# Attention scores from two 64-row halves of the TensorE array instead of 128-row products with q high and low stacked

## The reference, cut to what matters

```python
q, k, v = jnp.split(h @ wqkv, 3, axis=-1)          # 8 heads of 64
q = l2norm(q) * qs; k = l2norm(k) * ksc
q, k = rotary_xpos(q, k)
# local attention: a window of 128 queries sees its own 128 keys and the 128 before
sim = jnp.einsum('bhwid,bhwjd->bhwij', bq, bk)     # 64 products per score
attn = jax.nn.softmax(jnp.where(mask, -max, sim), axis=-1)
out = jnp.einsum('bhwij,bhwjd->bhwid', attn, bv)
```

## Time and profile before

| | |
|---|---|
| median of 3 runs | 3440.58 us (3440.16 to 3442.09) |
| span of the profiled execution | 3440.9 us (0.3 us above the median) |
| mean granted clock of PE | 0.976 of full |
| busy share PE / DVE / ACT / POOL | 93% / 86% / 67% / 55% |
| stretch of the loop over slots | about 860 to 3400 us |

### The profile page before, as it was taken

One profiled execution on the slowest core, in us unless ns is written; L12 is line 12 of the kernel. 1 busy time (PEld: TensorE's weight loads), 2 busy tenths in 40 slices (PEclk: granted clock), 3 DMA queues, 4 the chain that ended last, 5 costly groups with the idle time before them and its releaser, 6 DMA issues.

```text
span 3440.9 us, 85961 instructions
## 1 busy us (share of the span) xinstructions
PE 3200.0 (93%) x24600; PEld 2670.4 (78%) x24600; DVE 2975.0 (86%) x8121; ACT 2315.4 (67%) x5021; POOL 1876.9 (55%) x2307
## 2 busy tenths in 40 slices
PE   6999999973999999999999999999999999999997
PEld 3666667672888888888888888888888888888886
DVE  6888787857899989988989989998998999899995
ACT  5435353503787777777777777877777777777774
POOL 2433333335665655655655656666665566666662
PEclk9999999985999999999999999999999999999999
DMA  1111111134111111111111111111111111111111
GB/s 35 46 52 41 56 37 55 40 119 140 35 43 40 37 40 41 41 41 41 37 40 45 37 45 38 41 55 43 43 45 46 46 43 43 44 45 51 46 45 36
DMA packets 205536, 163.08 MB, mean 47 GB/s; under 512 B 25646, under 2 KB 203282, under 8 KB 204946
## 3 DMA queue, kind: packets, MB, share of 16 engines
q1 hardware_dynamic: 205330, 161.06, 15.3%
HBM read 106.44 MB, written 54.54 MB: 47 GB/s over the span
## 4 chain that ended last, share of the span: by engine, by line
DVE 24%; issue 18%; PE 18%; ACT 12%; POOL 1%; DVEq 1%; ACTq 1%; DMA 0%; SPq 0%; POOLq 0%
PE b_ps L898 4%; DVE b_probs L1173 4%; PE b_ps L948 3%; ACT b_probs L1021 3%; PE b_ps L870 2%; DVE b_kT_low L1123 2%; DVE b_probs L1160 2%; ACT b_gl L1036 2%; ACT L1021 2%; PE b_ps L886 2%; DVE b_qT L1120 2%; PE b_ps L913 2%; PE b_ps L914 2%; DVE b_t L1062 2%; ACT b_qT L987 2%
## 5 line engine op out<-in xcount | busy, mean ns | idle before, releaser
L870 PE MATMUL b_ps<-b_wqkv,b_hT_hi 128*128 128x512 f32 x1536 | 503.4, 409 | 43.2 <-DVE b_qT L1120 42.2
L1222 POOL TENSOR_TENSOR b_rstd<-b_var,b_mhalf 128x1 f32<-128x1 f32 x128 | 72.2, 564 | 821.1 <-DVE b_var L1134 821.1
L1021 ACT ACTIVATE b_probs<-b_probs,b_negmax 128x256 f32<-128x256 f32 x1024 | 505.6, 495 | 5.7 <-DVE b_negmax L1160 3.3
L948 PE MATMUL b_ps<-b_h2T,b_w 128*128 128x256 f16 x4224 | 474.2, 273 | 0.7 <-ACT b_h2T L979 0.7
L948 PEld LDWEIGHTS b_ps<-b_h2T,b_w 128*128 128x128 f16 x4224 | 414.5, 98 | 49.3 <-ACT b_h2T L979 0.9
L1212 POOL TENSOR_TENSOR b_sq<-b_sq 128x512 f32<-128x512 f32 (+5 forms) x768 | 418.1, 544 | 58.2 <-ACT b_sq L1000 17.9
L1173 DVE TENSOR_SCALAR b_probs<-b_probs,b_rinv 128x256 f32<-128x256 f32 x1024 | 424.8, 456 | 18.1
L1244 POOL TENSOR_TENSOR b_rn<-b_ss_min,b_mhalf 128x16 f32<-128x16 f32 x128 | 379.2, 2963 | 34.9 <-DVE b_ss_min L1071 33.3
L870 PEld LDWEIGHTS b_ps<-b_wqkv,b_hT_hi 128*128 128x128 f32 x1536 | 281.0, 193 | 114.8 <-DVE b_qT L1120 57.8
L442 PE MATMUL a_ps<-a_xs,a_E 128*128 128x256 f16 x3072 | 345.2, 273 | 4.1 <-POOL a_xs L233 4.0
L959 PE MATMUL b_ps<-b_w,b_hid 128*128 128x256 f32 x1536 | 342.2, 379 | 1.2 <-DVE b_hid L1196 1.2
(11 more groups left out here) (136 smaller groups left out, 7305.4 us busy)
## 6 DMA issues: line engine op xcount, KB each, us to landing
b_hx<-xs_dram SPq DMA_DIRECT2D x256, 64.0 KB, 1.9
b_rot<-rot_dram SPq DMA_DIRECT2D x128, 128.0 KB, 2.1
b_xr<-xs_dram SPq DMA_DIRECT2D x128, 128.0 KB, 2.1
xp_dram<-b_xp SPq DMA_DIRECT2D x128, 128.0 KB, 1.7
b_h<-xp_dram SPq DMA_DIRECT2D x256, 64.0 KB, 1.8
a_xn<-in_L_attn_x_dram SPq DMA_DIRECT2D x20, 512.0 KB, 3.8
a_x_res<-in_L_attn_x_dram SPq DMA_DIRECT2D x66, 128.0 KB, 2.1
x_dram<-a_x SPq DMA_DIRECT2D x64, 128.0 KB, 1.7
```

The source lines that it names most:

```text
L870: last = nc.tensor.matmul(ps[:, bank, :], hT[:, k, :], wqkv[:, ds(layer(s), 1), part, k, bank * INNER:(bank + 1) * INNER], start=(k == 0 a ...
L948: last = nc.tensor.matmul(ps[:, bank, half * 2 * P:(half + 1) * 2 * P], w1[:, ds(layer(2 * j), 1), wp, k, first:first + P], h2T[:, hp, k, ...
L1021: nc.scalar.activation(probs[:, h, :], probs[:, h, :], ACT.Exp, bias=negmax[:, h:h + 1], scale=-1.0, accum_out=rowsum[:, h:h + 1]).then_in ...
```

## The change

The high and low parts of q and k are kept in four full-width tiles, one entry for each pair of heads, with one head in the upper 64 partitions and the other in the lower. There is no stacking, no copy across halves, and no zeros. Each head's scores come from three products of 64 rows. The two heads of a pair are issued one after the other, one in the upper and one in the lower half of the array's rows, and they write to different PSUM banks. So the heads are placed anew: bank 3 holds heads 0 and 2, bank 4 heads 1 and 3, bank 5 heads 4 and 6, bank 6 heads 5 and 7, and PE reports scores after every second pair instead of every pair. Waits for the banks follow (`BANK_READ`).

```diff
+BANK_READ = {3: 3, 4: 4, 5: 7, 6: 8}
...
-            kT = sb("kT", [P, HEADS, 2 * P], F32R)
-            kT_low = sb("kT_low", [P, HEADS, 2 * P], F32R)
+            kT, kT_low = sb("kT", [P, HP, 2 * P], F32R), sb("kT_low", [P, HP, 2 * P], F32R)
...
-            qT = sb("qT", [P, HEADS, P], F32R)
+            qT, qT_low = sb("qT", [P, HP, P], F32R), sb("qT_low", [P, HP, P], F32R)
...
+            def head_scores(h):
+
+                bank, column = 3 + 2 * (h // 4) + h % 2, (h // 2) % 2
+                return ps[:, bank, column * 2 * P:(column + 1) * 2 * P]
...
-                        pe.wait_ge(kT_lo, 2 * (t + 1))
-                        pe.wait_ge(kT_both, 2 * (t + 1))
-                        pe.wait_ge(qT_lo, 2 * (t + 1))
+                        pe.wait_ge(kT_lo, t + 1)
+                        pe.wait_ge(qT_lo, t + 1)
                         for p in range(HP):
-                            for h in range(2):
-
-                                scores = ps[:, 3 + p, h * 2 * P:(h + 1) * 2 * P]
-                                nc.tensor.matmul(scores, qT[:, 2 * p + h, :], kT[:, 2 * p + h, :], start=True, stop=False)
-                                last = nc.tensor.matmul(scores, qT[:, 2 * p + h, :], kT_low[:, 2 * p + h, :], start=False, stop=True)
-                            last.then_inc(scores_done, 1)
+                            for a, (q_part, k_part) in enumerate(((qT, kT), (qT, kT_low), (qT_low, kT))):
+                                for h, rows in enumerate(half_rows):
+                                    last = nc.tensor.matmul(head_scores(2 * p + h), q_part[rows, p, :], k_part[rows, p, :], start=(a == 0), stop=(a == 2))
+                            if p % 2 == 1:
+                                last.then_inc(scores_done, 1)
...
-                        for h, rows in enumerate(half_rows):
-                            nc.scalar.copy(qT[rows, h::2, :], by_pair(ps[rows, 2, :])).then_inc(qT_hi, 1)
+                        nc.scalar.copy(qT[:], by_pair(ps[:, 2, :])).then_inc(qT_hi, 1)
                         act.wait_ge(kT_done, t + 1)
                         par = (r - 1) % 2
-                        for h, rows in enumerate(half_rows):
-                            nc.scalar.copy(kT[rows, h::2, par * P:(par + 1) * P], by_pair(ps[rows, 6, :])).then_inc(kT_hi, 1)
-                        for h, rows in enumerate(half_rows):
-                            act.wait_ge(kT_hi, 2 * t + h + 1)
-                            nc.scalar.copy(kT[half_rows[1 - h], h::2, par * P:(par + 1) * P], kT[rows, h::2, par * P:(par + 1) * P]).then_inc(kT_both, 1)
+                        nc.scalar.copy(kT[:, :, par * P:(par + 1) * P], by_pair(ps[:, 6, :])).then_inc(kT_hi, 1)
...
-                        for h, rows in enumerate(half_rows):
-                            dve.wait_ge(qT_hi, 2 * t + h + 1)
-                            nc.vector.tensor_tensor(qT[half_rows[1 - h], h::2, :], by_pair(ps[rows, 2, :]), qT[rows, h::2, :], ALU.subtract).then_inc(qT_lo, 1)
-                        for h, rows in enumerate(half_rows):
-                            dve.wait_ge(kT_hi, 2 * t + h + 1)
-                            nc.vector.tensor_tensor(kT_low[rows, h::2, par * P:(par + 1) * P], by_pair(ps[rows, 6, :]), kT[rows, h::2, par * P:(par + 1) * P],
-                                                    ALU.subtract).then_inc(kT_lo, 1)
+                        dve.wait_ge(qT_hi, t + 1)
+                        nc.vector.tensor_tensor(qT_low[:], by_pair(ps[:, 2, :]), qT[:], ALU.subtract).then_inc(qT_lo, 1)
+                        dve.wait_ge(kT_hi, t + 1)
+                        nc.vector.tensor_tensor(kT_low[:, :, par * P:(par + 1) * P], by_pair(ps[:, 6, :]), kT[:, :, par * P:(par + 1) * P],
+                                                ALU.subtract).then_inc(kT_lo, 1)
...
-                            wait_apart(dve, scores_done, HP * t + p + 1, passed_dve)
+                            if p % 2 == 0:
+                                wait_apart(dve, scores_done, 2 * t + p // 2 + 1, passed_dve)
```

More of the change, by code:

```diff
@@ L735, in phase_b @@
                 "kT_done", "qT_done", "kT_hi", "kT_lo", "qT_hi", "qT_lo"))
-            kT_both = sem("kT_both")
             scores_done, mask_ready = sem("scores_done"), sem("mask_ready")
@@ L862, in run @@
                             if bank == 2:
-                                wait(pe, qT_lo, 2 * s)
+                                wait(pe, qT_lo, s)
                             else:
@@ L882, in run @@
                             if p == HP - 1 and in_range(s - 1):
-                                pe.wait_ge(kT_lo, 2 * s)
+                                pe.wait_ge(kT_lo, s)
                             pe.wait_ge(probs_ready, HEADS * t + 2 * p + 2)
@@ L942, in run @@
                             if bank > 2 and in_range(s - 1):
-                                pe.wait_ge(scores_kept, HEADS * (s - 1) + 2 * (bank - 3) + 2)
+                                pe.wait_ge(scores_kept, HEADS * (s - 1) + BANK_READ[bank])
                             for half in range(1 if c == FULL else 2):
@@ L955, in run @@
                         if in_range(s - 1):
-                            pe.wait_ge(scores_kept, HEADS * (s - 1) + 2)
+                            pe.wait_ge(scores_kept, HEADS * (s - 1) + BANK_READ[3])
                         for n in range(2):
@@ L984, in run @@
                         act.wait_ge(qT_done, t + 1)
-                        wait(act, scores_done, HP * t)
-                        for h, rows in enumerate(half_rows):
-                            nc.scalar.copy(qT[rows, h::2, :], by_pair(ps[rows, 2, :])).then_inc(qT_hi, 1)
+                        wait(act, scores_done, 2 * t)
+                        nc.scalar.copy(qT[:], by_pair(ps[:, 2, :])).then_inc(qT_hi, 1)
                         act.wait_ge(kT_done, t + 1)
                         par = (r - 1) % 2
-                        for h, rows in enumerate(half_rows):
-                            nc.scalar.copy(kT[rows, h::2, par * P:(par + 1) * P], by_pair(ps[rows, 6, :])).then_inc(kT_hi, 1)
-                        for h, rows in enumerate(half_rows):
-                            act.wait_ge(kT_hi, 2 * t + h + 1)
-                            nc.scalar.copy(kT[half_rows[1 - h], h::2, par * P:(par + 1) * P], kT[rows, h::2, par * P:(par + 1) * P]).then_inc(kT_both, 1)
+                        nc.scalar.copy(kT[:, :, par * P:(par + 1) * P], by_pair(ps[:, 6, :])).then_inc(kT_hi, 1)
                     if in_range(s):
@@ L1157, in run @@
                                 floor_norms(s)
-                            wait_apart(dve, scores_done, HP * t + p + 1, passed_dve)
+                            if p % 2 == 0:
+                                wait_apart(dve, scores_done, 2 * t + p // 2 + 1, passed_dve)
                             for h in range(2 * p, 2 * p + 2):
-                                nc.vector.tensor_tensor_reduce(probs[:, h, :], ps[:, 3 + p, (h % 2) * 2 * P:(h % 2 + 1) * 2 * P], which,
+                                nc.vector.tensor_tensor_reduce(probs[:, h, :], head_scores(h), which,
                                                                rn[:, (r - 1) % 2, h:h + 1], ABOVE_ALL, ALU.add, ALU.min,
```

## The result

The changed kernel takes 3271.52 us (median of 4 runs, 3270.43 to 3272.43) against 3441.04 us, a ratio of 0.9507 with a 95% interval from 0.9494 to 0.9521. The forecast was 3302 us, and the range 3272 to 3392. The direction was right.

What follows compares the result with a forecast made beforehand. PE was taken as the bound, idle 105 us of its loop in short stalls that begin on DVE and ACT. Stalls of 102 us plus 36 us of score work made 138 us off 3440.9: 3302 us, range 3272 to 3392.

Steps and rivals of the forecast that it cites:

- The bound, and what each instruction costs: Loop: PE bounds with short stalls begun by DVE and ACT; a half-width cast or subtraction costs as much as full width.
- Halves at once: Score products: the two 64-row products of a pair run at once, 0.118 us a pair, with 0.235 as the other bound.
- the likeness to L898: Product with v, split by columns: two products run at once and loads run in pairs; taken as model for 0.118 us.
- rivals 1 and 2: Score pairs: halves take turns, 0.235 us a pair, 3484 us, chance 0.15; or overlap in part, 0.16, 3367 us, chance 0.10.
- The score block: Score products on PE: 1.72 us instead of 2.00, 0.28 less over 128 slots, 36 us gained.
- the second change of the array's division: From halves to the full array ahead of L837: new cost of 0.1 to 0.2 us, taken as 0.2.
- The jump: Loop jump: qkv product at L886 starts 1.47 us earlier after each of 31 jumps, 46 us gained.
- D: Time DVE begins L1120 after the loop's jump, 2004.51 in the trace; claimed to move along with PE.
- the even slots of the second layer: L886 in even slots not following a jump: 0.64 us of idle time and lost overlap, 14 times, 9 us gained.
- Odd slots: L886 to L898 and L898 itself: ACT's copies keep pace, 0.48 us in some 60 slots, 29 us gained.
- L837 in the second layer: Wait of L837 in odd slots: 0.6 us of idle time and lost overlap in 29 slots, 18 us gained.
- Rival 3: Whole loop: other waits replace those removed; with only half of the 102 us back, 3353 us; chance 0.13.

Runs made afterwards that it cites:

- e1: The changed kernel with all 12 score products of the upper rows issued first, then all 12 of the lower; 3401.12 us.
- g1: The changed kernel with 14 DVE semaphore increments ahead of the first loop and 24 between the loops, so only the first loop has the stop; 3267.76 us.
- f2: The changed kernel with 38 DVE semaphore increments between the two loops, none in a loop; no stop in either loop; 3254.65 us.
- e4: The changed kernel with 4 more DVE semaphore increments in every slot, 16 in each loop body and 32 ahead of the first; 3291.27 us.
- e2: The changed kernel with each DVE subtraction done for the two halves again; 3386.89 us.
- f1: The new score products alone: the changed kernel with DVE's subtractions and ACT's casts in halves again and two more ACT copies; 3398.23 us.
- f4: The kernel before with 100 DVE semaphore increments ahead of the first loop and 119 between the loops; only the second loop lost its stop; 3411.16 us.
- f3: The changed kernel with 14 DVE semaphore increments ahead of the first loop; stop in the first loop, two stops in the second; 3305.20 us.

## Why the prediction was wrong, by its steps

**The bound, and what each instruction costs: right.** PE is the bound, and it was found idle for 25 us, forecast near 30. A cast takes 587 ns in full width and took 582 in half width, a subtraction 690 and 689. No L994 is left, and L841 and L890 hardly wait for DVE.

**Halves at once: right**, and the likeness to L898 carried it. Pairs come every 0.113 or 0.118 us, e1 shows what turns would have cost, and rivals 1 and 2 are out. TensorEngine Tiling (Array Packing) of the Trainium skill says under Key Properties that tiles load and multiply in parallel. The trace agrees: the two loads of a pair begin 3 ns apart, and so do its two products. The 24 loads don't queue up. (The prediction calls 24 loads a third more than 16. They are half more; its sum doesn't use it.)

**The score block: right in kind, too small in size.** It is 1.61 us (median) and not 1.72. The mis-sized term is the second change of the array's division: from the last pair to the first product of L841 it takes 0.22 us, so about 0.1 beyond a pair's distance and not the 0.2 I put in. A pair was sized rightly. The block gives 47 us instead of 36.

**The jump: this is the step that failed.** The prediction said that DVE begins at D, 2.86 us late, and that D moves along with PE, and so it took the stop as fixed. In the first loop it went altogether. It depends on where the loop's body lies in DVE's program, and the change, with fewer DVE instructions ahead of that body and in it, left it without the stop. That is worth 13 us (g1 against f2). With the stop the change would have taken about 3285 us, inside the range. e4, which has both stops, takes 3291. Nothing of the rows before told of this, except that the 2.86 us had "issue" as their reason.

The sum of this step had a second error, which hid the first in part. I multiplied by 31 jumps, and there are 25; 25 x 1.47 is 37 us and not 46. Each jump gave more than 1.47, though. With both stops in place (e4), the qkv block behind a jump lost 1.63 us in the first loop and 1.75 in the second, 42 us in all. Without the first loop's stop it is 54. That 42 is near 46 is luck.

The stop alone is not the whole surplus of 32 us: the jumps give 8 more than forecast, odd and even slots 11 more, the score block 11 more, other blocks 2. Each term but those of L837 and of the even slots of the second layer (9 us, as forecast) was too small, and together they passed the lower end of the range.

**Odd slots: right in kind, too small.** Transposes and the product with v lost 0.40 + 0.16 us in odd slots, not 0.48, and 0.05 in even ones: 40 us in all against 29. Why the even ones got shorter isn't shown.

**L837 in the second layer: right.** Before, the score blocks of the second half took 145 us against 127 in the first; now they take 104 against 103. The 18 us of difference were forecast and are gone.

**Rival 3, stalls handed on: no.** But e2 shows that it was near. With the old work on DVE, 59 us of waits for the attention output came in place of the shorter score block. The prediction counted savings of DVE and ACT only against waits that stood in the profile before, and left out those that the faster PE would have made. The change brings the faster PE and the savings at once, so these waits never appear and the sum came near, though its account of what each part is worth was wrong: it gave the products 36 us by themselves, and alone they give 13 (f1 against f4).

## What to carry to other kernels

When one engine is dense and two others are close behind, sum up waits for the change as a whole; don't price its parts one by one, since each part's worth depends on the others (11 or 59 us for the same work on ACT). If a head's 64 channels leave half the array's rows empty, put the two heads of a pair into the row halves, with neighbouring instructions in different halves: grouped by half, the same products took 2.65 us instead of 1.61. (Here neighbours also write to different banks; no run varied that.) And where an engine stops behind a loop's jump with "issue" as the reason, try to move the body by some instructions before believing a comparison of one per cent: f2 and f3, the same loops moved by 38 and 14 instructions, lie 51 us or 1.5% apart.

## What the runs showed of the hardware that I had not expected

- DVE's stop behind a jump (2.5 us) depends on where the body lies in its program. The same body, 38 instructions on, had none; 14 instructions on it stopped twice, for 2.2 and 1.6 us. Each turn of the loop with a stop has five packets of 8 KB on the instruction queue, each turn without one has none (166, 99 and 39 packets for 25, 12 and 0 such turns).
- A pair of 64-row fp32r products with 256 moving columns, in different row halves, takes as long as a single one of 64 rows (e1) or of 128 rows (before): 0.113 or 0.118 us in each kind of block, means 0.116, 0.116 and 0.117. What decides between the two values is open.
- In e1 the first product of the second half began before the last two of the first half, which stand ahead of it in the program. The names in the rows show it in all 128 blocks: two of `b_kT,b_qT`, then two of `b_kT_low,b_qT`, then two of `b_kT,b_qT_low`.
